# Graph network on one core: an earlier gather index and another order of TensorE's work in two stages

## The reference, cut to what matters

```python
# layer 0 (stage mean_runs)
msg = feat[src] * e_feat
neigh_sum = segment_sum(msg, dst)
h_neigh = neigh_sum / maximum(deg, 1.0)[:, None]
rst = feat @ W_self.T + b_self + (h_neigh @ W_neigh.T + b_neigh)
x = layernorm(x + rst)
# layer 1, first convolution (stage first_gate)
k, q, v = x @ Wk, x @ Wq, x @ Wv
msg = sigmoid(k[dst] + q[src]) * v[src]
h = relu((segment_sum(msg, dst) + x @ Ws + b) @ Wl1 + bl1)
```

## Time and profile before

| what | value |
| --- | --- |
| median of 3 runs | 9893.81 us (9874.47 to 9901.17) |
| the profiled execution, its own time | 9912.28 us |
| its span | 9910.6 us |
| PE / DVE / ACT / POOL busy, whole span | 5129.8 / 6701.4 / 3997.7 / 6515.3 us |
| stage mean_runs | about 1405 to 2597 us |
| stage first_gate | about 3156 to 3874 us |

### The profile page before, as it was taken

How to read it: one execution, slowest core, us unless ns; L and a number is a source line. 1 busy time by engine, 2 the same in 40 slices (tenths; PEclk the granted TensorE clock), 3 DMA queues, 4 the chain that set the end, 5 groups by cost and what they waited for, 6 DMA issues and landing times. The chain is left out here.

```text
span 9910.6 us, 128475 instructions
## 1 busy us (share of the span) xinstructions
PE 5129.8 (52%) x22317; PEld 4085.5 (41%) x22317; DVE 6701.4 (68%) x16290; ACT 3997.7 (40%) x10116; POOL 6515.3 (66%) x6395
## 2 busy tenths in 40 slices
PE   5220026666444665444477776666666566652222
PEld 1000015555333443222266666665666555442222
DVE  5766767777787555565588888888999745543333
ACT  1667845555322222444444444444545333321111
POOL 0776756666576555777666666665555577767777
PEclk9555557777655555555566666666666666665555
DMA  3000024444322343333311111112233344442222
GB/s 135 8 8 23 7 57 132 132 132 133 77 49 59 90 92 85 83 84 85 73 37 38 38 37 38 37 37 88 97 99 97 96 136 138 138 125 62 61 60 49
DMA packets 825286, 757.17 MB, mean 76 GB/s; under 512 B 451844, under 2 KB 567882, under 8 KB 821802
## 3 DMA queue, kind: packets, MB, share of 16 engines
q1 hardware_dynamic: 637068, 589.29, 19.6%
q0 software_dynamic: 188160, 167.28, 9.0%
HBM read 458.34 MB, written 309.38 MB: 77 GB/s over the span
## 5 line engine op out<-in xcount | busy, mean ns | idle before, releaser
L2646 DVE CUSTOM_DVE_ANT_0 att_junk<-bank,att_away 128x512 f32<-128x512 f32 x1568 | 977.9, 683 | 121.0 <-PE bank L2826 107.9
L996 PE MATMUL bank<-att_payload,att_match 128*128 128x68 f32 x3136 | 582.0, 365 | 198.6 <-issue 100.4
L996 PEld LDWEIGHTS bank<-att_payload,att_match 128*128 128x128 f32 x3136 | 570.4, 280 | 243.3 <-issue 243.3
L2585 POOL DMA_INDIRECT attn_tab<-att_new,att_put_i x392 | 387.3, 988 | 409.6 <-DVE att_new L2683 317.2
L1045 POOL DMA_INDIRECT ga_ends<-x_tab,ga_src_i x392 | 410.4, 1047 | 302.2 <-issue 253.0
L472 POOL DMA_INDIRECT half_sorted<-ka_out_row,ka_put_i x392 | 397.9, 1015 | 284.3 <-ACT ka_put_i L605 169.3
L1045 POOL DMA_INDIRECT ma_ends<-in_x,ma_src_i x392 | 397.3, 1013 | 262.6 <-ACT ma_dst_i L1037 157.9
L675 POOL DMA_INDIRECT edges<-kb_out_row,kb_put_i x392 | 423.5, 1080 | 154.3 <-issue 122.7
L3667 PE MATMUL bank<-ident,sb_pay 128*65 128x128 f32 x392 | 109.4, 434 | 747.4 <-DVE sb_pay L3554 747.4
L1615 POOL DMA_INDIRECT x_tab<-mb_run,mb_put_i x392 | 400.7, 1022 | 143.0 <-issue 97.0
L1045 POOL DMA_INDIRECT sa_ends<-x_tab,sa_dst_i x392 | 390.4, 996 | 152.8 <-issue 139.2
(11 more groups left out here) (505 smaller groups left out, 19446.4 us busy)
## 6 DMA issues: line engine op xcount, KB each, us to landing
da_agg<-attn_tab SPq DMA_DIRECT2D x98, 288.0 KB, 2.9
attn_tab<-ka_attn_start SPq DMA_DIRECT2D x24, 1152.0 KB, 29.0
x_tab<-ma_wide SPq DMA_DIRECT2D x98, 260.0 KB, 2.1
ma_xn<-in_x SPq DMA_DIRECT2D x98, 256.0 KB, 3.1
h_tab<-ma_h_out SPq DMA_DIRECT2D x98, 256.0 KB, 2.1
attn_x<-ma_z_out SPq DMA_DIRECT2D x98, 256.0 KB, 2.7
ga_same<-same_next SPq DMA_DIRECT2D x196, 128.0 KB, 3.0
gb_same<-same_prev SPq DMA_DIRECT2D x98, 256.0 KB, 3.4
```

The source lines that it names most:

```text
L996: ins = self.nc.tensor.matmul(bank[:, u * w:(u + 1) * w], self.match[s][:, t, u * P:(u + 1) * P], self.payload[s][:, t, :], start=(t == 0) ...
L2585: nc.gpsimd.indirect_dma_start(st["attn_tab"], bass.IndirectOffsetOnAxis(ap=put_i[s][:, q:q + 1], axis=0), new[s][:, q, :], None, bounds_c ...
L2646: ins = nc.vector.tensor_tensor_reduce(junk[h % 2][:, q, :], logit_t[h % 2][:], away[s][:, q, :], 1.0, -2.0 * BIG, ALU.subtract, ALU.max, ...
```

## The change

In mean_runs: ScalarE's `index` is called for the block three ahead, behind `pay` of the next block, and no longer for the block two ahead at the head of the step; ScalarE's `one_node.copy` stands ahead of the roots; `label` moves ahead of `pay`, and `copy` ahead of `widen`. TensorE's step begins with `first_turns`, then does `mix`, the next chunk's `one_node.multiply` and the next block's `turn`, and then all of this chunk's network (`h_turns`, `h_hide`, `h_rows`, `z_multiply`), which before was mixed with them. Gather index 2 is written ahead of the loop.

In first_gate: TensorE's step turns the block three ahead first (before: two ahead), then does `produce` of the block two ahead and `mix` of the next, as before. ScalarE's step calls `copy` and `open_gate` for the block two ahead as before, then `locate` for the block three ahead and `index` for the block five ahead (before: `index` four ahead at the head, `locate` two ahead at the end). SyncE loads near rows four ahead. The work ahead of the loops follows, and ScalarE has six steps behind its loop instead of four. No instruction's shape and no buffer is changed.

```diff
 mean_runs, scalar
             def step(n, i, s, first, last):
                 more = there(n + 1, BLOCKS)
-                if there(n + 2, BLOCKS):
-                    index(*ahead(n, i, s, 2))
-                n_root(n)
-                if not fresh(n):
-                    z_take_root(n - 2)
                 if more:
                     one_node.copy(act, n + 1, first_turn)
+                n_root(n)
+                if not fresh(n):
+                    z_take_root(n - 2)
                 if not fresh(n, 1):
                     take_root(n - 1, i + s - 1, 1 - s)
+                label(n, i, s)
                 if more:
                     pay(*ahead(n, i, s, 1))
+                if there(n + 3, BLOCKS):
+                    index(*ahead(n, i, s, 3))
                 h_copy(n)
-                label(n, i, s)
-                widen(n, i, s)
                 if more:
                     copy(*ahead(n, i, s, 1))
+                widen(n, i, s)
                 h_relu(n)
 mean_runs, tensor
+                if more:
+                    first_turns(*ahead(n, i, s, 1))
                 mix(n, i, s)
                 if more:
-                    first_turns(*ahead(n, i, s, 1))
+                    one_node.multiply(pe, n + 1, first_out, st["w_pair"][0][:])
+                    turn(*ahead(n, i, s, 1))
                 h_turns(n, s)
-                if more:
-                    turn(*ahead(n, i, s, 1))
                 h_hide(n)
-                if more:
-                    one_node.multiply(pe, n + 1, first_out, st["w_pair"][0][:])
                 h_rows(n)
                 z_multiply(n)
 first_gate, sync
+                if there(n + 4, BLOCKS):
+                    load_near(*ahead(n, i, s, 4))
                 if there(n + 3, BLOCKS):
-                    load_near(*ahead(n, i, s, 3))
                     load_near_same(*ahead(n, i, s, 3))
 first_gate, scalar
-                if there(n + 4, BLOCKS):
-                    index(*ahead(n, i, s, 4))
                 if there(n + 2, BLOCKS):
                     copy(*ahead(n, i, s, 2))
                     open_gate(*ahead(n, i, s, 2))
-                    locate(*ahead(n, i, s, 2))
+                if there(n + 3, BLOCKS):
+                    locate(*ahead(n, i, s, 3))
+                if there(n + 5, BLOCKS):
+                    index(*ahead(n, i, s, 5))
 first_gate, tensor
+                if there(n + 3, BLOCKS):
+                    turn(*ahead(n, i, s, 3))
                 if there(n + 2, BLOCKS):
-                    turn(*ahead(n, i, s, 2))
                     produce(*ahead(n, i, s, 2))
                 if there(n + 1, BLOCKS):
                     mix(*ahead(n, i, s, 1))
 ahead of the loops
+            index(2, 1, 0)            # mean_runs, scalar
+            load_near(3, 1, 1)        # first_gate, sync
+            locate(2, 1, 0)           # first_gate, scalar
+            index(4, 2, 0)
+            over_pairs(act, BLOCKS, step, tail=6)
+            turn(2, 1, 0)             # first_gate, tensor
```

More of the change, by code:

```diff
@@ L1462, in step @@
                 more = there(n + 1, BLOCKS)
-                if there(n + 2, BLOCKS):
-                    index(*ahead(n, i, s, 2))
+                if more:
+                    one_node.copy(act, n + 1, first_turn)
                 n_root(n)
@@ L1467, in step @@
                     z_take_root(n - 2)
-                if more:
-                    one_node.copy(act, n + 1, first_turn)
                 if not fresh(n, 1):
                     take_root(n - 1, i + s - 1, 1 - s)
+                label(n, i, s)
                 if more:
                     pay(*ahead(n, i, s, 1))
+                if there(n + 3, BLOCKS):
+                    index(*ahead(n, i, s, 3))
                 h_copy(n)
-                label(n, i, s)
-                widen(n, i, s)
                 if more:
                     copy(*ahead(n, i, s, 1))
+                widen(n, i, s)
                 h_relu(n)
@@ L2022, in _ @@
                 index(2 + s, 1, s)
-            over_pairs(act, BLOCKS, step, tail=4)
+            locate(2, 1, 0)
+            index(4, 2, 0)
+            over_pairs(act, BLOCKS, step, tail=6)
         @block.tensor
```

## The result

The changed kernel takes 9718.0 us (median of 4 runs, 9715.8 to 9720.8) against 9897.5 before (median of 4 runs too, the three of the table above and one more): ratio 0.9815, 95% interval 0.9802 to 0.9827, 180 us less. The forecast was 9676, 42 us too low; the result lies inside the stated range, and both stages went the way that was forecast.

A forecast was written before the change was run, and what follows sets the result against it. Bounds: in mean_runs a TensorE and VectorE ring alternating with the late index, in first_gate the gather's ring through locate. Savings 136 + 82 = 218 us, from 9912.28 to 9694, less 18.5 for the median: 9676; range 9650 to 9790.

The forecast's parts named there:

- What bounds first_gate, and the size of the win: first_gate: landing to next gather falls from 6.52 to 4.77 us, 1.75 a pair; stage 82 us less.
- the ring: first_gate: gather, landing, turn, scan, produce, sigmoid, locate, next gather into that slot; 14.29 us for two blocks.
- Rival D: mean_runs: landing late by as much as index was early, nothing gained; first_gate gains nothing either; 9890 us, chance 0.04.
- Rival B: first_gate wins nothing: landing awaited at head of TensorE's step holds produce as long as saved; 9758 us, chance 0.07.
- Two rings of nearly equal length in mean_runs: mean_runs: a TensorE and VectorE ring of 11.7 us a block takes turns with the late index holding the gather.
- GpSimd as the bound after: mean_runs: after the change GpSimd's gathers and their issue set the block, at least 10.38 us.
- rival A: mean_runs: TensorE's network row bounds at a clock under 0.65; block 11.4 to 12.3 us, total 9763 to 9851, chance 0.13.
- I add 0.12: 10.5 us: mean_runs: 0.12 us added to 10.38 for gathers beside VectorE and slow blocks; block 10.5 us, 136 us less.
- Rival C: mean_runs: two-SBUF-input VectorE instructions hold gathers for their full length, 3.3 us a block; total 9948 us, chance 0.04.

The follow-up runs named there:

- f_turn: Changed kernel, but first_gate's ScalarE order as before while TensorE still turns three ahead: 10262.2 us, ratio 1.0352 to the kernel before.
- f_locate: Changed kernel's mean_runs; first_gate as before except locate moved up two lines, ahead of copy and open_gate: 9667.3 us, ratio 0.9755 to the kernel before.
- m_index: Kernel before with only mean_runs' index moved, to three ahead behind pay: 9865.4 us, ratio 0.9945.
- m_order: Kernel before with only mean_runs' new TensorE and ScalarE order, index still two ahead at the head: 9881.9 us, ratio 0.9963.
- again: The changed kernel unaltered, run again on one chip with three other runs: 9714.9 us, ratio 0.9817 to the kernel before.
- f_head: Changed kernel with first_gate's locate (three ahead) and index (five ahead) at the head of ScalarE's step: 9634.4 us, ratio 0.9714 to the kernel before.

## Why the prediction was right, and where it was off

- **What bounds first_gate, and the size of the win.** Right, term by term: turn to gather 4.66 us where 4.70 was forecast, the pair shown 12.4 and the mean one 12.7 where 12.5 was. That the stage gave 82 us, the forecast to the microsecond, is partly luck: the same code of before differs by up to 16 us between three traces (702.5, 693.7, 686.6). f_turn and f_locate show that the ring runs through locate, as the prediction says. What it did not say is that the earlier turn gains nothing by itself, and that locate(m) needed no sigmoid at all.
- **Rival D** (nothing changes) did not come. **Rival B** (the landing at the head of TensorE's step takes it back): not so in the changed kernel; in f_turn, where locate stays behind, it is the whole result.
- **Two rings of nearly equal length in mean_runs.** Right, shown by m_index and m_order: 11.4 and 11.6 us alone. The prediction's 11.7 for the first was 0.3 too long, and it gave the second no length.
- **GpSimd as the bound after.** Right: its idle time is its issue. **TensorE's row as the bound** (rival A) did not come: the clock is 0.80. Single blocks at 1.2 GHz do show: VectorE waits for `ma_first_root` 36 times, 1.3 us at most, with a mean granted clock of 0.54 in the 8 us before such waits and 1.0 before the others. GpSimd waits for TensorE's turn only 4.3 us in the whole stage, so they are made good, as gathers run ahead.
- **The step that was mis-sized: "I add 0.12: 10.5 us".** The block is 10.88, 0.38 above. The gathers are 8 x (1.032 - 0.998) = 0.28 longer, and GpSimd pauses six times for 2.1 to 3.6 us, 18.3 us in all, which is 16.5 beyond the usual 0.30 each, or 0.17 a block. The prediction had no term for these, though the trace of before has six too, of 2.25 us; less the 0.12 allowed that is 0.33 of the 0.38. This term is 0.38 x 97 = 37 of the 42 us. The other 5: the profiled execution of before lay 18.5 us above the median of its three runs and that of after 2.8, which is 15.7; against it the profiled execution fell by 191.5 us, 10.5 more than the two stages give.
- **Rival C** (two-input instructions hold a gather): the mechanism is there and the price was wrong. It took every such instruction for a full hold, 3.3 us; the rows give 8 x (1.032 - 0.94) = 0.7 us, since only a gather that starts inside one is held, and only for the rest. By the Trainium skill (SBUF — State Buffer, "SBUF: two separate sides"), whichever of the two starts first gets the shared pair of ports for its whole instruction, and the other waits. The trace agrees for the gather: one that starts second is held to the end, and one already running loses nothing (0.94). It does not show the other half: VectorE's instruction that starts second, inside a running gather, takes 0.69 to 0.72 us, no longer than elsewhere by more than 0.03.

## What to carry to other kernels

When a ring with a gather in it sets a stage, ask of each of its members whether it needs what stands ahead of it in its engine's queue: the copy of one column stood behind a sigmoid it never read, and with that one line moved, first_gate's gathers were 54 us shorter than with the whole change. Where an engine waits in turns for two things, price both rings before trusting either: relieved one at a time they gave 0.5 and 0.3 us a block, together 1.0. And moving one engine's work ahead without its partner's can serialise what was double-buffered: it cost 544 us here.

## What the runs showed of the hardware that I had not expected

- A gather that starts t us before the end of a VectorE instruction with two SBUF inputs takes about t - 0.12 us longer in mean_runs (0.62 gave 0.51, 0.53 gave 0.41); in first_gate's scan L1946 after the change the longest takes 0.93 longer; one that starts in an instruction with one SBUF input or none takes 0.94.
- With 0.4 to 0.7 us of VectorE work a block added, the stage was 0.3 to 0.4 us a block shorter than in again (10.82); what moved the gathers' starts is open, as said above.
- GpSimd pauses once in 112 gathers in mean_runs (counted between two pauses of after; 14 blocks of eight), before the change as well as after, and also in first_gate (before, after and f_head, there 149 to 153 us apart). Two of before, then two of after:

```profile
1738.18 0.94 POOL L1045 DMA_INDIRECT ma_ends<-in_x,ma_src_i  x1 [2.25 <-issue]
1905.24 0.94 POOL L1045 DMA_INDIRECT ma_ends<-in_x,ma_src_i  x1 [2.25 <-issue]
```

```profile
1553.50 0.94 POOL L1045 DMA_INDIRECT ma_ends<-in_x,ma_src_i  x1 [2.92 <-issue]
1706.74 0.94 POOL L1045 DMA_INDIRECT ma_ends<-in_x,ma_src_i  x1 [3.58 <-issue]
```

Nothing that the profile shows releases it, and it falls between two gathers of one block. Its cause was not tried.
